# A small vision transformer on one core: three pixel buffers, value products of 256 columns, and the experts' gates applied before the down product

## The reference, cut to what matters

```python
# tokens: 196 patches of 768 values per image
x = layernorm(patches) ; x = x @ W_proj + b_proj ; x = layernorm(x)
h = concat([cls_tok, concat([cls, x]) + pos_embedding])            # 64 x 198 x 192
# attention: 12 heads of 64, relative positions on keys and on values
qkv  = layernorm(h) @ qkv_w.T
attn = softmax((q k + q r_p_k) * scale) ; out = attn v + attn r_p_v
h = h + out @ proj_w.T + proj_b
# experts: one shared MLP and 8 gated ones of 192 hidden units, the best 2 of 8 per token
xf = layernorm(h)
scores = sigmoid(xf @ router_w.T) ; combine = normalised scores of the top 2, 0 elsewhere
hid = square(relu(einsum('nc,ech->neh', xf, w1))) ; y = einsum('neh,ehc->nec', hid, w2)
h = h + shared(xf) + einsum('nec,ne->nc', y, combine)
```

## Time and profile before

| | us |
|---|---|
| median of 3 runs | 4823.09 (4813.13 to 4823.2) |
| the profiled execution | 4822.31 |
| its span | 4820.6 |
| PE busy in the span | 4384.5 (91%) |
| DVE busy | 3036.6 (63%) |
| ACT busy | 2333.0 (48%) |
| POOL busy | 1228.3 (25%) |

### The profile page before, as it was taken

One profiled execution on the slowest core, in us unless ns is written; L12 is line 12 of the kernel. 1 busy time (PEld: TensorE's weight loads), 2 busy tenths in 40 slices (PEclk: granted clock), 3 DMA queues, 4 the chain that ended last, 5 costly groups with the idle time before them and its releaser, 6 DMA issues. The chain is left out here.

```text
span 4820.6 us, 91022 instructions
## 1 busy us (share of the span) xinstructions
PE 4384.5 (91%) x30810; PEld 4248.1 (88%) x30810; DVE 3036.6 (63%) x8013; ACT 2333.0 (48%) x6372; POOL 1228.3 (25%) x1418
## 2 busy tenths in 40 slices
PE   4777499899999999999989999999996899999999
PEld 4777399899899989989989989989995899999999
DVE  3556456666666656656665666666664677777776
ACT  2444366566566556656656666655662222222221
POOL 2112222122122222222212212212221333333333
PEclk8888699999999999999999999999997999999999
DMA  6442200000000000000000000000001000000000
GB/s 140 110 100 60 53 1 1 1 21 1 1 22 1 1 2 22 1 2 21 1 1 22 1 1 22 1 1 3 10 1 38 13 20 19 15 20 20 17 17 20
DMA packets 65161, 99.53 MB, mean 21 GB/s; under 512 B 3763, under 2 KB 60674, under 8 KB 61120
## 3 DMA queue, kind: packets, MB, share of 16 engines
q1 hardware_dynamic: 61312, 90.31, 7.4%
q0 software_dynamic: 944, 2.42, 0.3%
q10 hardware_dynamic: 2560, 2.36, 0.2%
HBM read 65.88 MB, written 29.20 MB: 20 GB/s over the span
## 5 line engine op out<-in xcount | busy, mean ns | idle before, releaser
L595 POOL TENSOR_TENSOR att_prob<-att_prob,att_total 99x396 f32<-99x396 f32 x768 | 650.0, 846 | 2400.9 <-DVE att_total L838 2400.9
L846 DVE TENSOR_REDUCE att_npeak<-att_s 99x2 f32<-99x396 f32 x768 | 436.4, 568 | 910.2 <-PE att_s L1015 908.3
L668 ACT ACTIVATE att_probT<-att_t 99x396 f32<-99x396 f32 x768 | 384.5, 501 | 947.7 <-PE att_t L984 945.2
L998 PE MATMUL att_o<-att_probT,att_vx 99*96 99x198 f32 (+1 forms) x3072 | 673.8, 342 | 33.6 <-DVE att_rx L831 32.7
L1015 PE MATMUL att_s<-att_kx,att_qx 96*99 96x198 f32 (+1 forms) x3072 | 655.3, 336 | 8.3 <-issue 5.8
L680 ACT ACTIVATE att_prob<-att_s,att_npeak 99x198 f32<-99x198 f32 x1536 | 635.2, 423 | 29.1 <-DVE att_npeak L846 26.7
L1383 PE MATMUL ffn_y<-ffn_down,ffn_hidden 128*128 128x192 f32 x3564 | 633.9, 328 | 4.7 <-DVE ffn_acc L1295 2.8
L1383 PEld LDWEIGHTS ffn_y<-ffn_down,ffn_hidden 128*128 128x128 f32 x3564 | 585.0, 190 | 26.4 <-DVE ffn_acc L1295 25.4
L1161 POOL TENSOR_TENSOR ffn_hidden<-ffn_relu 128x384 f32<-128x384 f32 x462 | 378.8, 826 | 704.7 <-ACT ffn_relu L1190 397.9
L998 PEld LDWEIGHTS att_o<-att_probT,att_vx 99*96 99x96 f32 (+1 forms) x3072 | 498.9, 181 | 65.8 <-issue 34.1
L1015 PEld LDWEIGHTS att_s<-att_kx,att_qx 96*99 96x99 f32 (+1 forms) x3072 | 515.4, 168 | 23.4 <-issue 9.4
(11 more groups left out here) (201 smaller groups left out, 9003.9 us busy)
## 6 DMA issues: line engine op xcount, KB each, us to landing
tok_pixels<-in_x SPq DMA_DIRECT2D x24, 1568.0 KB
ffn_hid<-hidden SPq DMA_DIRECT2D x34, 288.0 KB, 2.9
att_xres<-hidden SPq DMA_DIRECT2D x8, 1188.0 KB
hidden<-att_xres SPq DMA_DIRECT2D x8, 1188.0 KB
out_hidden<-ffn_acc SPq DMA_DIRECT2D x33, 288.0 KB, 2.3
hidden<-tok_rows SPq DMA_DIRECT2D x8, 1176.0 KB
att_oT<-in_L_attn_qkv_w ACTq DMA_DIRECT2D x1, 1536.0 KB, 11.2
tok_posb<-in_L_tok_pos_embedding POOLq DMA_DIRECT2D x1, 1176.0 KB, 42.1
```

What stands on the lines that cost most here:

```text
L595: nc.gpsimd.tensor_tensor(prob[:, i % 2, :, :], prob[:, i % 2, :, :], view(total[:, i % 2, :], [[1, 2], [0, NTOK]]), ALU.mult).then_inc(pr ...
L668: nc.scalar.activation(probT[:, i % 2, :], t_bank[0:HALF, 0:2 * NTOK], ACT.Copy).then_inc(probT_made, 1)
L846: nc.vector.tensor_reduce(npeak[:, i % 2, :], s_bank[i % 2][0:HALF, 0:2 * NTOK].rearrange("p (h k) -> p h k", h=2), AX.X, ALU.max, negate= ...
L998: ins = nc.tensor.matmul(o_bank[0:M, 0:NTOK], vx[:, p % 2, 2 * b + k, v0:v0 + M], probT[:, j % 2, k * NTOK:(k + 1) * NTOK], start=(k == 0) ...
```

## The change

It has three parts, one in each stage.

**Tokens.** SLOTS = 3 pixel buffers: SP issues the loads of three groups at the start, and the load for g+3 when group g's buffer has been read. The loops over pairs of groups are written out as eight groups, and the last group leaves out the statistics of a group after it.

**Attention.** The values of two pairs are made at once: tiles of 256 columns, two per job (VALUES = 8 jobs per two pairs, in place of 4 of four tiles per pair). The copy of the values, vx, has one place instead of two, so ACT waits before it overwrites it until the products of the pair before (outs) with those images are done, and PE waits for the bank's release before it uses them. Even pairs carry 24 first jobs, odd ones 16, and spread has another order.

**Experts.** DVE multiplies the hidden units by the gates before the down product (gate_hidden). The down products of all 14 chunks then add up in one bank per tile, and a chunk that two experts share is multiplied once (42 products per block instead of 54). The gates are needed with the tokens along the columns and the same on all partitions: PE turns them, ACT copies them, SP stores them to DRAM (gate_rows) and reads each expert's row back to 128 partitions, in two halves. All relus are on ACT. Residuals are loaded into acc by DMA. Hidden units and split inputs have two places.

```diff
-        pixels = m.sb("pixels", [P, 2, CH, XROW])
+        pixels = m.sb("pixels", [P, SLOTS, CH, XROW])
...
-                load(0, 0)
-                load(1, 1)
-                with sp.Fori(0, (GROUPS - 2) // 2) as pair:
-                    gg = pair * 2
-                    for s in range(2):
-                        sp.wait_ge(normed_made, (gg + s + 1) * SIDE)
-                        load(gg + s + 2, s)
-                        store(gg + s, s)
...
+                for g in range(SLOTS):
+                    load(g)
+                for g in range(GROUPS):
+                    if g + SLOTS < GROUPS:
+                        sp.wait_ge(normed_made, (g + 1) * SIDE)
+                        load(g + SLOTS)
+                    store(g, g % 2)
...
-        vx = m.sb("vx", [HALF, 2, TILES, 160])
+        vx = m.sb("vx", [HALF, TILES, 2, 160])
...
-        COST = {"turn": [10] * TURN, "first": [9] * 8 + [8, 8, 8, 5] + [8, 8, 8, 4] + [18] * 4,
+        COST = {"turn": [10] * TURN, "first": [9] * 8 + [8, 8, 8, 5] + [8, 8, 8, 4] + [10] * VALUES,
...
+                        if v != "opening":
+                            act.wait_ge(outs, g * STEPS + (p - 1) * UNIT + 2 * b + 2)
                         ins = nc.scalar.activation(
-                            view(vx[:, s, 4 * (j - 16):4 * (j - 15), :], [[160, 4], [96, 2], [1, HD]]),
+                            view(vx[:, 2 * b:2 * b + 2, :, :], [[160, 4], [96, 2], [1, HD]]),
                             view(bank[0:HALF, :], [[128, 4], [HD, 2], [1, HD]]), ACT.Copy)
...
-                        for t in range(4):
-                            cols = slice((4 * (j - 16) + t) * HALF, (4 * (j - 16) + t + 1) * HALF)
-                            out = bank[0:HALF, t * 128:(t + 1) * 128]
+                        for t in range(2):
+                            cols = slice((2 * (j - FIRST) + t) * HALF, (2 * (j - FIRST) + t + 1) * HALF)
+                            out = bank[0:HALF, t * 256:(t + 1) * 256]
...
-                                ins = nc.tensor.matmul(out, x[:, cols], w[:, 2, weights, :],
+                                ins = nc.tensor.matmul(out, x[:, cols], w[:, 2, weights:weights + 2, :],
...
+                    if j >= 0 and p % 2 == 0 and head == 0:
+                        k = order[v]["first", p, FIRST + b]
+                        pe.wait_ge(free[k % RING], through(base, v, "first", p, FIRST + b, k % RING) + PRIMED)
...
+                def spread_gates(k, s):
+
+                    sp.wait_ge(gateT_made, k + 1)
+                    sp.dma_start(gate_rows[s, :, :], gateT[:, :]).then_inc(gate_stored, 16)
+                    sp.wait_ge(gate_stored, k * 16 + 16)
+                    for h in range(2):
+                        half = EXPERTS // 2
+                        src = gate_rows[s, half * h:half * (h + 1), :]
+                        sp.dma_start(gates[:, s, half * h:half * (h + 1), :],
+                                     bass.AP(tensor=src.tensor, offset=src.offset, ap=[[0, 128], [BT, half], [1, BT]])
+                                     ).then_inc(gates_in[s][h], 16)
...
-                            nc.vector.scalar_tensor_tensor(acc[:, s, t, :], y, gate[:, s, t, e:e + 1], acc[:, s, t, :],
-                                                           ALU.mult, ALU.add).then_inc(summed, 1)
...
+                    halves = {0: ((0, 128, 2 * i),), 1: ((0, 64, 2 * i), (64, 128, 2 * i + 1)), 2: ((0, 128, 2 * i + 1),)}[c]
+                    for lo, hi, e in halves:
+                        ins = nc.vector.tensor_tensor(hidden[lo:hi, s, j, :], hidden[lo:hi, s, j, :], gates[lo:hi, s, e, :], ALU.mult)
+                    ins.then_inc(gated, 1)
...
+                        for n in range(SHARED, SHARED + AHEAD):
+                            gate_hidden(it, pair, s, n)
+                        for n in range(HT):
+                            if SHARED <= n and n + AHEAD < HT:
+                                gate_hidden(it, pair, s, n + AHEAD)
+                            if n in PARTS:
+                                route(it + 1, st, [n - PARTS[0]])
+                            if n == STATS:
                                 dve.wait_ge(hid_in[s], pair * 16 + 32)
                                 statistics(s, st)
-                            if k == 7:
+                            if n == NORM:
                                 layernorm(it + 2, s, st)
+                            if n == TURNS:
+                                low(it + 2, s)
+                        sums(it, pair, s)
...
-                            ins = nc.tensor.matmul(y_bank[t][:, 0:DIM], hidden[:, j, t * 128:(t + 1) * 128],
-                                                   down[:, e, i, :], start=(i == 0), stop=(i == len(parts) - 1))
+                        ins = nc.tensor.matmul(y_bank[t][:, 0:DIM], hidden[:, s, j, t * 128:(t + 1) * 128],
+                                               down[:, j, :], start=(n == 0), stop=(n == HT - 1))
```

More of the change, by code:

```diff
@@ L303, in _ @@
+                    assert st.n == (PER_GROUP if more else PER_GROUP - 2), st.n
             @block.tensor
@@ L446, in first_jobs @@
         def first_jobs(p):
-            return [("first", p, j) for j in range(FIRST)]
+            return [("first", p, j) for j in range(FIRST + (VALUES if p % 2 == 0 else 0))]
         def last_jobs(p):
@@ L1069, in experts_stage @@
         mv_made, sd_made = m.sem("mv_made"), m.sem("sd_made")
-        expo, sc, sb_, eq, first, left, second, weight = (m.sb(n, [128, TB, EXPERTS]) for n in (
-            "expo", "score", "biased", "eq", "first", "left", "second", "weight"))
-        gate = m.sb("gate", [128, 2, TB, EXPERTS])
+        expo, sc, sb_, eq, first, left, second, weight, gate = (m.sb(n, [128, TB, EXPERTS]) for n in (
+            "expo", "score", "biased", "eq", "first", "left", "second", "weight", "gate"))
         top = m.sb("top", [128, TB, 1])
@@ L1075, in experts_stage @@
         h_bank = [m.bank(f"h{i}") for i in range(2)]
[L1076 removed]
+        y_bank = [m.bank(f"y{i}") for i in range(TB)]
         r_bank = m.bank("r")
@@ L1183, in relus @@
[L1183 to L1190 removed]
+                    nc.scalar.activation(x0h[:, s, :], t_bank[0][:, 0:BT], ACT.Copy)
@@ L1197, in _ @@
[L1197 removed]
+                for n in range(HT):
+                    relu_of(0, 0, n)
+                turned_gates(0)
                 deviation(1)
[L1199 to L1206 removed]
+                high(1, 1)
@@ new lines, in _ @@
+                with act.Fori(0, (BLOCKS - 1) // 2) as pair:
+                    for s in range(2):
+                        it = pair * 2 + s
+                        for n in range(HT):
+                            relu_of(it + 1, 1 - s, n)
+                            if n == STATS:
+                                deviation(it + 2)
+                            if n == GATES:
+                                turned_gates(it + 1)
+                            if n == TURNS:
+                                high(it + 2, s)
@@ L1224, in layernorm @@
                     st.settle()
+                    if not isinstance(k, int) or k:
+                        dve.wait_ge(turned, k)
                     for t in range(TB):
```

440 lines of the change are left out of this document (233 added, 207 removed).

## The result

| | median us | range | ratio to the kernel before (95%) |
|---|---|---|---|
| before | 4818.11 | 4810.22 to 4823.2 | |
| changed | 4538.66 | 4526.56 to 4546.2 | 0.9419 (0.939 to 0.9448) |

The forecast was 4520 in a range of 4460 to 4615. The profiled execution of the changed kernel took 4544.49 us with a span of 4542.5. Two starts cut each span into three stages: the first score product of attention and the last one of its last group.

A forecast was written before the change was run, and what follows sets the result against it. PE was taken to bound attention (95% busy) and experts (99%), while the tokens wait for pixels. From 4822.3 us, tokens -69, attention -105 and experts -132 gave 4516, stated as 4520, range 4460 to 4615.

The forecast's parts named there:

- "no gain" rival: Attention: value products of 256 columns cost twice those of 128, giving 4627 us; chance 0.08.
- Sum of stalls per group: Attention: net change of PE's waits per group, summed to -1.6 us, taken as +0.25, so +2 in eight groups.
- the bound of +5: Attention: upper bound on the change of PE's stalls per group, in us; the lower was -2.
- the projection's +5.4: Attention: PE waits before the projection for DVE's copy in four more pairs, 1.35 us each, +5.4 us per group.
- The -4 for L943: Attention: waits before the first row table shrink 1.0 us each, as value or key jobs come between; -4 us per group.
- The -3: Attention: turning jobs keep most of their wait, but one of three per group falls apart; -3 us per group.
- The waits eat attention's gain: Attention: projection waits in all pairs and shorter ring jobs add 9 us per group, giving 4590 us; chance 0.10.
- The down products' 3.90: Experts: 84 down instructions per block instead of 108, at 0.1625 us each, save 3.90 us.
- The cover: Experts: gate work stays hidden; products at 0.60 us, DVE 18.9 of 28.1 us, gates landing 4.1 us into the next block.
- The slack of 4 us: Experts: DVE's chain ends at 20.9 us, PE turns the norm at about 25, so all is hidden by 4 us.
- The rival in which DVE sets the block: Experts: products of 1.0 us or gates 4 us later make the norm late; block 30.5 us, total 4597; chance 0.15.
- The slower case, gates read at 28 GB/s: Experts: spreading gates to 128 partitions takes 56 us, blocks about 60, time near 5500 us; chance 0.04.

The follow-up runs named there:

- The variants: The changed kernel with attention's jobs reordered: later projection 4468.14 us; also later row product 4478.0; later projection with filled steps 4417.86; then turning jobs in twos 4401.77.

## Why the prediction came out right, and where it was wrong

**Tokens, right in mechanism and size.** Forecast -69, measured -70.1. Taking the period from the one group that didn't wait, and not the 13 us of the wait, was what made it exact; the DMA kept up, at 122 GB/s over the window. The two-buffer run ties it to the buffer.

**The width, right.** 0.120 taken, 0.118 measured; the width alone is worth 111 us by its spacings and 129 in the run that undoes it, most of the difference by the clock. The "no gain" rival is excluded. The Trainium skill ("TensorE: Matmul & The Clock Gate", section "Back-to-back issue gap") gives 109 ns for an isolated product by its formula, and some 98 by an estimate between its sustained figures. The trace's 118 is 8 and 20% above these; it was above both at 128 and 384 columns too.

**Attention's waits, the step that failed.** "Sum of stalls per group -4 + 5.4 - 3 = -1.6 ... I take +0.25." PE's idle time over the stage rose by 46 us, +5.8 a group, above the bound of +5. Of the three terms: the projection's +5.4 was right in kind and too small, as the mean wait is 80.5/46 = 1.75 us and not the 1.35 taken (L817 stands behind all of a step on DVE). The -4 for L943 did not hold: that wait did go, but the row product that stands in the same step took it over (32.6 us against 32.0). The -3 did not come: the query products' 53.6 us are 50.2. I had priced each wait as a property of two neighbours. The variants show it as a property of the step: one output bank, and DVE that needs a fixed time per step.

A term is missing as well: the sum prices every product at the full clock. The waits brought more time at the lower level (123 to 164 us), about 20 us by estimate, so that PE's busy time fell by 95 us and not 111. That the waits pull the clock down is read from where the stretches begin and from the variants, in which both fall together; no run here changes one alone. "The waits eat attention's gain" was the rival for this, with 70 us lost and 0.10; 56 us were lost, and it deserved more.

**Experts, right in mechanism, gain too small.** Block 27.42 against 28.1. The down products' 3.90 were right. What was mis-sized is the waits: I took 0.4 us a block off for them, and all of the 1.2 us that the block had beyond its instructions went. The three turns of the gates cost 0.33 instead of 0.26. Together -3.90 + 0.33 - 1.2 makes the 4.8 us between 32.18 and 27.42. What the stage gained beyond its blocks, put at 1 to 2 us, is some 7 by subtraction.

**The cover, right in sign, with wrong parts.** Gated products 0.71 instead of 0.60, DVE 20.5 instead of 18.9 us a block, but the gates 4 us earlier than I had them: the two errors offset each other, which is luck. The slack of 4 us is 2.4 to 5.0 by the run with the gates twice. The rival in which DVE sets the block would have needed that much more over 16 products, so 0.86 us or more each. The slower case, gates read at 28 GB/s, is far off: 768 KB in 5.1 us.

**The order of the jobs** was costed as given. That another one is worth 137 us, more than the whole attention part brought, is the finding that the prediction's reading missed. Over the stage 99 us of it are PE's idle time (201 to 101) and 47 its busy time (2827 to 2780) at a clock that falls less (164 us to 51).

## What to carry to other kernels

Where one engine runs a fixed step and extra jobs are laid between, look at the shortest step, not at neighbours: a wait removed by moving a job can come back at the next meeting with the slow engine unless the step is filled. Read the granted clock beside the waits: here a wait cost more than its own length. When a buffer removes a wait, take the gain from a period that has no wait, and when gates or scales move into an engine with idle time, measure its slack by doubling the work, as its idle time of 7 us a block overstates it here (2.4 to 5.0).

## What the runs showed of the hardware that I had not expected

- A product of two SBUF operands on DVE takes 0.555 us for 384 columns with POOL mostly idle, on 64 partitions as on 128, and one of 1736 columns takes 1.968. A line through the two, an estimate, is 0.15 us fixed and 1.05 ns a column; scaling the long one down loses the fixed part.
- POOL slows as well: its squares of 128 x 384 take 0.826 us before, 0.909 with 16 gated products a block on DVE, and 0.983 with 32.
- A matrix product of 256 columns against 99 weight columns starts every 0.118 us, one of 128 every 0.088, and one of 384 against 128 weight columns every 0.175: 0.23 ns a column from 128 to 256, and 0.45 from there to 384.
- In the changed kernel 18 of the 38 stretches at the lower clock in attention follow a PE wait of 1.5 to 2.6 us before one product, the projection. There four score products took 1.53 us instead of 0.83.
- The gates' halves, 768 KB each, read from DRAM rows to 128 partitions, land in 5.1 us, and at 90 GB/s of DMA traffic PE stays busy for the whole window.
